# Moving the output projection of the previous chunk ahead of the head loop in a Mamba-2 scan kernel

## The reference

```
xn = layernorm(x)
h  = xn + mamba2_mixer(rmsnorm(xn) * norm_w)         # the scan below, with in_proj ahead of it
a  = h + down(silu(gate(rmsnorm(h))) * up(rmsnorm(h)))
out = x + a + ffn_int8(xn)

# in mamba2_mixer: 32 heads of 64 channels, state of 128
def step(h, inputs):
    dA_t, dt_t, B_t, x_t, C_t = inputs
    dBx = einsum('bh,bn,bhp->bhpn', dt_t, B_t, x_t)
    h = h * dA_t[:, :, None, None] + dBx
    y = einsum('bhpn,bn->bhp', h, C_t)
...
y = y + D * x
y = rmsnorm(y * silu(z), ssm_norm_w)
return einsum('ble,de->bld', y, out_proj_w)
```

## Time and profile before

| | us |
|---|---|
| median of 2 runs | 4448.33 (4404.47 and 4492.2) |
| the profiled execution's own time | 4408.1 |
| its span on the slowest core (core 1) | 4406.6 |
| spans of the 8 cores | 4391.0 to 4406.6 |
| granted TensorE clock, mean by core | 0.723 to 0.728 of full |

### The profile page before, as it was taken

The page is one execution under the profiler, slowest core; times in us unless marked ns, Lnnn a source line. Parts: engine busy times, 40 slices in busy tenths (PEclk is TensorE's granted clock), DMA queues, the critical chain, the costliest instruction groups (busy, mean ns, idle before and its releaser), DMA issues.

```text
span 4406.6 us, 36502 instructions; the slowest of 8 cores (4391.0 to 4406.6 us)
## 1 busy us (share of the span) xinstructions
PE 2304.2 (52%) x9681; PEld 1027.5 (23%) x9681; DVE 1796.6 (41%) x3928; ACT 556.8 (13%) x1011; POOL 156.0 (4%) x160
## 2 busy tenths in 40 slices
PE   0526424435673333333433433777777746778777
PEld 0212202212231111111111111333333312333333
DVE  3534575646425656565655541222222201222222
ACT  3000120001023212121112110111111100000000
POOL 0110000000010000000000000000000000000000
PEclk9998765557886555555555556788888867889988
DMA  6562000011121311111111119000000084111111
GB/s 169 190 163 61 19 0 1 1 41 22 19 70 41 91 48 52 49 48 53 44 58 39 63 42 151 20 20 24 24 20 20 15 137 87 34 34 50 34 34 36
DMA packets 94289, 234.09 MB, mean 53 GB/s; under 512 B 23984, under 2 KB 26832, under 8 KB 93456
## 3 DMA queue, kind: packets, MB, share of 16 engines
q0 software_dynamic: 40448, 106.44, 11.1%
q1 hardware_dynamic: 51344, 116.94, 8.6%
q10 hardware_dynamic: 2304, 8.39, 0.7%
HBM read 235.13 MB, written 51.66 MB: 65 GB/s over the span
## 4 chain that ended last, share of the span: by engine, by line
PE 43%; DVE 20%; issue 15%; DMA 12%; ACT 5%; POOL 1%; DVEq 1%; another core or an unknown queue 1%; SPq 0%; ACTq 0%; POOLq 0%
PE P L1082 4%; PE P L1245 4%; PE P L1249 4%; DMA wu<-w_u 4%; PE P L689 3%; PE P L478 3%; PE P L1086 3%; PE P L483 3%; DMA bcast<-lam_dram 3%; DVE Emt L868 2%; PE P L1285 2%; PE PS L1285 2%; PE PS L659 2%; PE P L1124 2%; PE PS L1124 2%
## 5 line engine op out<-in xcount | busy, mean ns | idle before, releaser
L874 PE MATMUL P<-x_tok,Emt 128*128 128x64 bf16 x512 | 108.3, 212 | 285.1 <-DVE Emt L868 264.6
L430 DVE SCALAR_TENSOR_TENSOR B_acc<-xbc,c_convw,B_acc 128x2048 bf16<-128x2048 bf16 x108 | 245.4, 2346 | 0.0
L1267 DVE TENSOR_TENSOR F_h<-F_h,P 128x1024 bf16<-128x1024 bf16 x48 | 58.6, 1221 | 386.8 <-ACT F_h L1261 386.8
L1104 DVE TENSOR_TENSOR E_h<-E_h,P 128x1024 bf16<-128x1024 bf16 (+1 forms) x48 | 53.3, 1110 | 381.7 <-ACT E_h L1098 381.7
L859 ACT ACTIVATE Est<-Est 128x128 f32<-128x128 f32 x512 | 154.9, 308 | 369.8 <-DVE Est L853 368.4
L1245 PE MATMUL P<-wg,F_xf 128*128 128x512 bf16 x384 | 149.4, 389 | 84.0 <-ACT F_h L1261 42.1
L478 PE MATMUL P<-xfh,wbuf 128*128 128x512 bf16 x288 | 114.4, 397 | 148.2 <-DVE wbuf L454 126.5
L332 PE MATMUL P<-c_identf,A_n 128*128 128x128 f32 x256 | 90.5, 445 | 193.3 <-DVE A_n L320 161.5
L1082 PE MATMUL P<-wg,E_hnT 128*128 128x512 bf16 x384 | 146.2, 404 | 81.4 <-ACT E_h L1098 61.3
L659 PE MATMUL PS<-c_ident,yn 128*128 128x128 bf16 x128 | 33.8, 264 | 289.9 <-DVE yn L943 253.7
L868 DVE SCALAR_TENSOR_TENSOR Emt<-Est,dtk,Gm 128x128 bf16<-128x128 f32 x512 | 175.9, 346 | 10.1 <-PE P L874 6.9
(11 more groups left out here) (197 smaller groups left out, 4327.0 us busy)
## 6 DMA issues: line engine op xcount, KB each, us to landing
bcast<-lam_dram SPq DMA_DIRECT2D x64, 512.0 KB
A_x<-x_own SPq DMA_DIRECT2D x32, 512.0 KB, 3.8
A_x<-x_pre SPq DMA_DIRECT2D x32, 512.0 KB, 4.0
wd<-w_d POOLq DMA_DIRECT2D x2, 5376.0 KB, 65.5
wg<-w_g POOLq DMA_DIRECT2D x5, 2048.0 KB, 43.1
wu<-w_u POOLq DMA_DIRECT2D x5, 2048.0 KB, 49.8
xn_dram<-A_n POOLq DMA_DIRECT2D x16, 512.0 KB, 4.6
xfh<-xfp_dram SPq DMA_DIRECT2D x4, 2048.0 KB, 15.5
```

What stands on the lines that cost most here:

```text
L430: e.scalar_tensor_tensor(a[:, :], xbc[:, ec * CW + k:ec * CW + k + T], self.c["convw"][:, ec * 4 + k:ec * 4 + k + 1], a[:, :], ALU.mult, A ...
```

## The change

`emit_tail(ch - 1)` is called behind `xw` and before the matmul for `Gm`, no longer behind the head loop. Nothing in it is altered. Line numbers from L820 to L880 grow by two; those from L883 on stay.

```diff
@@ -816,6 +816,8 @@
             vxw = self.op("vector", lambda e, dw=dw_: e.tensor_tensor(
                 xw[:, :], x_tok[:, :], exp64(dw), ALU.mult),
                 wait=[("sv", A["vdw"]), ("sv", t_btok)], inc=("sv", 1))
+            if not pre and (ch - 1) in pend_tail:
+                emit_tail(ch - 1)
             if not pre:
                 mg = self.op("tensor", lambda e, W0=W0: e.matmul(
                     slotB_f[:, 0:128], xbc[:, 16 * CW + 3 + W0:16 * CW + 3 + W0 + Q],
@@ -878,8 +880,6 @@
                                                  if h == 0 else []),
                             inc=("st", 1))
                 t_mt_last = t_mth[NH - 1]
-                if (ch - 1) in pend_tail:
-                    emit_tail(ch - 1)
                 ev_y = self.op("vector", lambda e: e.tensor_tensor(
                     y_acc[:, :], y_acc[:, :], P0[:, :], ALU.add),
                     wait=[("st", t_mt_last), ("sv", ez)], inc=("sv", 1))
```

## The result

| | before | after |
|---|---|---|
| median of the runs | 4450.03 us (10 runs) | 4360.8 us (11 runs) |
| the profiled execution's own time | 4408.1 us | 4360.22 us |
| spans of the 8 cores | 4391.0 to 4406.6 us | 4338.2 to 4358.7 us |

The ratio is 0.9896, with a 95% interval of 0.9881 to 0.9911; against the 4408.1 us that the forecast starts from, it stands for 46 us (39 to 52). The two profiled executions differ by 47.9 us. A program on all eight cores is in some executions slowed on one die (cores 0 to 3 or 4 to 7) or on both, at a lower granted clock; the ratios of this document leave these runs out, the medians of its tables don't.

A forecast was written before the change was run, and what follows sets the result against it. Stage-by-stage waits, not a busy engine, were taken to bound the kernel. Per chunk 2.3 + 2.9 - 2.7 = 2.5 us, 37 us for 15 chunks, took 4408.1 us to 4371 us; range 4325 to 4412.

The forecast's parts named there:

- the model chunk: The one chunk of the earlier trace for which all terms were made, then multiplied by 15 moved tails.
- (a): Tail ahead of `Gm` on TensorE: starts at about 2110.2, takes 9.6 us; `xw` covers 2.3 us of VectorE's wait.
- (b): `Gm` and first `y_acc` behind the tail: four matmuls take 0.9 us, in time; L838 starts 8.4 us later.
- (c): Behind the head loop: L883 no longer comes after the tail, 2.3 us a chunk saved.
- (d): GpSimd's product L886 runs early, so L890 follows L883 after 2.46 us, not 5.35: 2.9 us a chunk saved.
- (e): Start of the head loop: VectorE's SBUF operations stand still until GpSimd's product L886 ends, 2.7 us a chunk lost.
- no hold: Rival: GpSimd's product beside the head loop costs nothing; 5.2 us a chunk saved, 4330 us; chance 0.13.
- only L868 is held: Rival: in the head loop L853 passes, L868 loses 1.9 us; 3.3 us a chunk saved, 4358 us; chance 0.13.
- GpSimd's next instruction holds too: Rival: issuing the `sz_t` load behind L886 also holds VectorE's loop, 0.6 us more lost; 4380 us; chance 0.09.
- `bcast` was not late: Sign against the forecast: `bcast` arrives late because the DMAs of `h1_t` and `sz_t` now run in the head loop.
- The low clock: Rival: TensorE's clock stays at 0.50, the tail takes 13.5 us; 2.0 us a chunk lost, 4438 us; chance 0.05.

The follow-up runs named there:

- e4: Kernel before, tail in its old place, GpSimd's product recorded ahead of the tail and waiting for the head loop's last L868; ratio 0.9896.
- e1: Changed kernel with GpSimd's product recorded ahead of the tail, so that it starts when x_tok is complete; median 4313.9 us, ratio 0.9765.
- e2: Kernel before, tail in its old place, with GpSimd's product recorded right behind `xw`; median 4480.3 us, ratio 1.0007.
- e3: Changed kernel with GpSimd's product waiting also for the head loop's ninth product on VectorE, so it lies inside the loop; median 4378.1 us, ratio 0.9931.
- e7: Changed kernel where the first L855 of each head loop writes its result to PSUM instead of SBUF; median 4467.7 us (two runs).
- e5: Kernel before, the tail's 32 matmuls spread one behind each head's matmul, GpSimd's product waiting for the loop's last VectorE product; median 4232.8 us, ratio 0.9589.

## Why the prediction was right, and where it was off

The forecast was 4371 us for the change; the changed kernel's profiled execution took 4360.22 us. By the forecast's steps, all in the model chunk:

- **(a) The tail in front of `Gm`.** L689 started 0.38 us after the last transpose did, forecast 0.42. Its length was the term that was mis-sized: 8.96 us, where I took 9.6. L697 started 9.21 us after it instead of 9.8. Over 15 chunks the mean of that distance is 9.1 to 9.3 us on the eight cores, and 9.5 to 9.7 before.
- **(b) `Gm` and L840.** The four matmuls took 1.03 us as the row counts them, forecast 0.9, and were in time. L840 started 0.20 us after `Gm`, not 0.28. From the last transpose to L840 it is 2097.15 - 2086.22 = 10.93 us, before 3.19: the shift is +7.7, forecast +8.4.
- **(c) Nothing behind the loop.** 3.0 us saved instead of 2.3, by the shift of (b) alone.
- **(d) GpSimd's product free early.** 5.35 to 2.46 us, exactly the 2.9 forecast. e4 shows it as a gain of its own.
- **(e) The hold.** From the start of L840 to that of L883 it is 2123.88 - 2097.15 = 26.73 us, where 2137.04 - 2112.97 = 24.07 would be without a tail: 2.66 us, forecast 2.7. Taking `xw` as the nearest row was right, although `xw` is seven times as long. e1, e2 and e3 each put the hold elsewhere and got about the size that it gives.

The sum is 3.0 + 2.9 - 2.7 = 3.2 us a chunk, 48 us, for the 47.9 us measured between the two profiled executions; the forecast had 2.5 and 37. The whole difference is in (a) and (b), 0.6 and 0.1 us.

Of the rivals, "no hold" (4330) and "only L868 is held" (4358) are out by the trace, though the second lies closer to the measured time than the forecast does: the first L855 of each loop was held, and a held L855 is what it excludes. This is why a time alone doesn't decide between mechanisms. "GpSimd's next instruction holds too" is out: VectorE went on 0.1 us after L886's end, beside L923. `bcast` was not late: the idle time before the first operation of each head is 51.9 us in all, and 53.3 before the change. The low clock did not stay: in the tail's first 4 us it was 0.50 and from then on 1.00:

```profile
2086.50:2090.50 4.00, 3.90 (x10) 1.41 (x11) 2.52 (x2) 0.00 (x0) 0.00 (x0) 0.50 0.00 0
2090.50:2095.50 5.00, 5.00 (x26) 2.29 (x25) 0.00 (x0) 0.00 (x0) 0.00 (x0) 1.00 0.00 0
```

Why the tail is shorter there is not settled. Against the earlier trace rows the clock rose some 0.6 us sooner after the tail's start. But the tail's new place is not shown to be the cause. The last tail did not move, and it too is shorter, 9.48 us against 9.86, and by 0.3 to 0.6 us on each of the eight cores:

```profile
2573.66 9.48 PE L689 MATMUL P<-wout,ynT 128*128 128x512 bf16 x32 [0.69 <-DVE ynT L663]
```

With the other tails in their old place, the means from first matmul to L697 are 9.3 to 9.4 us in e2 and 9.1 to 9.3 in e4 (cores 4 to 7); in the new place they are 9.4 to 9.6 in e7, and within the one execution of e1 single tails range from 8.1 to 10.4 us over its cores. There is one trace of each kernel, so it stays open how much of the mean belongs to a kernel and how much to an execution. It is not only the traced execution that gained more than was forecast: the ratio's interval is 39 to 52 us, all of it above 37.

The Trainium skill's page "SBUF — State Buffer", section "Who interferes with whom", named the condition that the rows before the change could not: VectorE operations with two SBUF inputs, and one-input operations in a two-port mode. Both agree here: L870 (two inputs) held for 4.13 us in e3, L855 (one input, SBUF to SBUF) for 2.95 us, and the same operation writing to PSUM (e7) not at all, 0.34 us. That the mode is the reason for the last, and not some other effect of a PSUM output, no run here shows; the runs show only which instructions are held.

## What to carry to other kernels

When a wait is moved, look for what stands behind the moved instructions on every queue they touch: here the worth of the move was a GpSimd product that had stood behind a DMA issue, and e4 gets it without the move. Then ask what the freed instruction will run beside; here GpSimd's product held every VectorE operation that started beside it and read and wrote SBUF alone, and none that read or wrote PSUM, so such a product belongs beside VectorE's idle time or its PSUM operations, and a held instruction shows as a long one, not as idle time. And an exposed wait of one engine may be worth more when it is spread over the time in which the engine it waits for is mostly idle than when it is moved: with the same instructions e5 takes 4% off the kernel before, 3% of it by the spreading and 1% by the product's place.

## What was not expected of the hardware

- A VectorE instruction of 128 columns that reads and writes SBUF waits out the whole rest of GpSimd's product, 2.66 to 3.8 us for 0.3 us of work; in no chunk did one slip in before the product's end.
- In the interleaved loop of e5 TensorE's clock stayed at its lower level. In this stretch, one matmul of 128x512 and one of 128x64 for each head, TensorE is recorded busy for 17.02 of 20.00 us, and the granted clock (the column behind POOL's) is 0.50:

```profile
2022.00:2042.00 20.00, 17.02 (x56) 4.11 (x56) 16.57 (x60) 9.12 (x30) 0.00 (x0) 0.50 0.24 80
```

It cost VectorE's loop nothing: at 1.2 GHz the two matmuls fit into the 0.66 us that VectorE needs for a head, and it got through 30 heads in these 20 us.
